# A GRU behind an attention layer: attention regrouped into units of four heads, steps begun after 32 tokens, feed-forward last

## The reference

```python
y   = gelu(x @ W.T + fc_bias + low_rank(f, x) + cond)            # (4, 256, 128)
q, k, v = y @ Wq, y @ Wk, y @ Wv                                  # 16 heads of 64
s   = (q.k + q.rel_emb[clip(i - j, -64, 64) + 64]) / 8            # position term per (i, j)
x   = x + (softmax(s) @ v) @ Wo + bo
# GRU over the 256 tokens, 4 sequences side by side
z   = sigmoid(x_t @ W_z + h @ U_z + cond @ C_z + b_z)
r   = sigmoid(x_t @ W_r + h @ U_r + cond @ C_r + b_r)
hh  = tanh(x_t @ W + (r * h) @ U + cond @ C + b)
h   = (1 - z) * h + z * hh                                        # history H
# feed-forward: the best of 8 experts of width 64 per token, rw = sigmoid(top logit)
out = x + sum_e mask_e * ((rw*H @ up_e.T) * silu(rw*H @ gate_e.T)) @ down_e.T
```

## Time and profile before

| | |
|---|---|
| median of 3 runs | 716.01 us (714.69 to 716.34) |
| span of the profiled execution | 712.3 us |
| median less that span | 3.7 us |
| busy PE, PEld | 623.2, 511.6 us |
| busy DVE, ACT, POOL | 461.2, 323.5, 177.9 us |
| mean granted PE clock | 0.973 |

### The profile page before, as it was taken

How to read it: one execution, slowest core, us unless ns; L and a number is a source line. 1 busy time by engine, 2 the same in 40 slices (tenths; PEclk the granted TensorE clock), 3 DMA queues, 4 the chain that set the end, 5 groups by cost and what they waited for, 6 DMA issues and landing times.

```text
span 712.3 us, 26221 instructions
## 1 busy us (share of the span) xinstructions
PE 623.2 (87%) x7909; PEld 511.6 (72%) x7909; DVE 461.2 (65%) x3362; ACT 323.5 (45%) x1253; POOL 177.9 (25%) x789
## 2 busy tenths in 40 slices
PE   5998888879888898989898989898888889999995
PEld 3445766658778777777787877777777677777864
DVE  1434666636777777777777777777766567766763
ACT  2355666623455555455555554555442223232221
POOL 1012444402332332333332323333211011111110
PEclk8999999977999999999999999999999999999996
DMA  8022555420222222222222222222210000000000
GB/s 231 3 82 59 145 154 140 132 67 25 74 74 69 66 66 66 66 71 71 68 70 68 66 66 66 67 75 66 74 25 2 2 2 6 7 5 4 5 8 6
DMA packets 47805, 43.08 MB, mean 60 GB/s; under 512 B 9340, under 2 KB 47496, under 8 KB 47624
## 3 DMA queue, kind: packets, MB, share of 16 engines
q1 hardware_dynamic: 47168, 40.76, 21.6%
q10 hardware_dynamic: 584, 1.64, 0.7%
HBM read 20.95 MB, written 21.43 MB: 59 GB/s over the span
## 4 chain that ended last, share of the span: by engine, by line
PE 59%; DVE 18%; issue 13%; ACT 7%; DMA 1%; DVEq 1%; SPq 1%; ACTq 0%; POOLq 0%; POOL 0%
PE bank L627 13%; PE bank L640 13%; PE bank L428 7%; PE bank L412 7%; DVE s_sb L850 4%; DVE o_sb L873 3%; ACT hh L770 3%; PE bank L445 2%; DVE g L1001 2%; DVE q L993 2%; ACT oT L656 2%; PE bank L460 2%; PE bank L532 2%; PE bank L462 2%; PE bank L458 2%
## 5 line engine op out<-in xcount | busy, mean ns | idle before, releaser
L360 POOL COPY x_nat<-d 128x4 f32 (+1 forms) x256 | 53.5, 209 | 391.8 <-DVE d L1006 391.8
L640 PE MATMUL bank<-q,uc 128*128 128x54 f32 (+1 forms) x512 | 106.2, 289 | 43.4 <-DVE q L993 41.0
L640 PEld LDWEIGHTS bank<-q,uc 128*128 128x128 f32 x512 | 77.7, 190 | 90.5 <-DVE q L993 85.8
L627 PE MATMUL bank<-g,uw 128*128 128x54 f16 (+1 forms) x2560 | 118.9, 189 | 3.6 <-DVE g L1001 3.6
L760 ACT ACTIVATE trz<-bank 128x8 f32<-128x8 f32 x256 | 45.5, 178 | 167.5 <-PE bank L627 167.2
L627 PEld LDWEIGHTS bank<-g,uw 128*128 128x128 bf16 x2560 | 103.3, 97 | 17.0 <-DVE g L1001 7.8
L627 PE MATMUL bank<-b,uw 128*128 128x54 f16 (+1 forms) x2560 | 110.1, 188 | 0.0
L627 PEld LDWEIGHTS bank<-b,uw 128*128 128x128 bf16 x2560 | 108.1, 103 | 1.1 <-issue 0.2
L770 ACT ACTIVATE hh<-bank 128x4 f32<-128x4 f32 x256 | 44.4, 174 | 135.6 <-PE bank L640 131.2
L1001 DVE TENSOR_TENSOR g<-z,hh 128x4 f16<-128x4 f32 x256 | 41.9, 164 | 97.4 <-ACT hh L770 97.4
L325 POOL COPY qa<-qT 64x64 f32 (+1 forms) x256 | 60.6, 237 | 102.3 <-PE bank L403 63.4
(11 more groups left out here) (133 smaller groups left out, 1025.4 us busy)
## 6 DMA issues: line engine op xcount, KB each, us to landing
skew<-e_sb SPq DMA_DIRECT2D x128, 159.5 KB, 2.2
pos<-skew SPq DMA_DIRECT2D x256, 64.0 KB, 2.4
wkv_sb<-in_L_attn_Wkv ACTq DMA_DIRECT2D x1, 1024.0 KB, 8.3
x_nat<-in_x SPq DMA_DIRECT2D x1, 512.0 KB, 4.5
wq_sb<-in_L_attn_Wq ACTq DMA_DIRECT2D x1, 512.0 KB, 6.0
wo_sb<-in_L_attn_Wo SPq DMA_DIRECT2D x1, 512.0 KB, 7.5
out<-y_out SPq DMA_DIRECT2D x8, 64.0 KB
ffn_nat<-in_L_ffn_w_gate SPq DMA_DIRECT2D x1, 256.0 KB
```

The lines of the kernel that those rows point to most:

```text
L627: ins = mm(out_, uw[:, gate, use, j, :], operand, start=False, stop=True, skip_group_check=True)
L640: mm(c_cols(k, n), uc[:, :], st["q8"][:, now, 0:n], start=False, stop=True, skip_group_check=True).then_inc(c_pre, 1)
```

## The change

Nearly the whole program is new. What it does:

1. **Weights multiplied ahead.** For each head a, M_a = Wq_a Wk_a^T and VO_a = Wv_a Wo_a (128 x 128 each) are formed once. The scores are then (y M_a) y^T, and the output is (P y) VO_a. The 48 projections, kT and v_sb are gone; what is projected, is projected per 32 tokens ("fills", below).
2. **Units of four heads and 32 tokens** of one sequence: 8 chunks x 4 quads of heads x 4 sequences = 128 units (`unit`). P is scaled by 1/sum before it is transposed (`normalize`). Positions read q, scores read g = y M, both straight from the layout of the fills: the POOL copies qa and qb are gone. Slanted loads are one DMA a unit.
3. **Fills.** Per chunk: 2 of q, 4 of g, 4 of o (the output product); each is 4 fp32 products of 128 columns in one spare bank, placed by a table at 40 places of 16 turns, and emptied by DVE in halves.
4. **Turns.** A turn carries unit n: scores(n), transposes and values of n-1, positions(n+4). Turns -4 to 19 run alone, with the late setup between them (transposes of y and Wv, the VO products, the feed-forward weights); step 0 begins at turn FIRST = 20, when 32 tokens of all sequences are done. From there a turn goes beside two steps, so units end at step 216 and the last output fill at step 222.
5. **A step.** r and z have a bank and a tanh each; no splits, all products fp32 with 4 columns: U_r g and U_r b (the older term, issued in the step before) into r, U_z h into z, U q into c. DVE has q, b, g and the state, which it writes into the history itself; POOL has no part in the steps.
6. **Feed-forward last**: 8 tiles of 32 tokens x 4 sequences, 9 slots each, from step FFN_STEP = 223 on; the last begins after step 255. The gate is ACT's Silu with rw as its scale, in place of tanh and products on DVE. Zero products (`fillers`) are put in only where neither attention nor a tile has work on PE.

```diff
-SPLIT = 4096.0
-PERIOD = 16
-EARLY = 5
-WIDE_BESIDE, WIDE = 54, 60
+CH = 32
+QUADS = 4
+UNITS = QUADS * B
+N_UNITS = NCH * UNITS
+LEAD = 4
+FIRST = 20
+FFN_STEP = 2 * (LAST_TURN - FIRST) + 1
+TILE_STEPS = 9
+PERIOD = [("o", -1, 3), ("q", 1, 0), ("q", 1, 1), ("o", 0, 0), ("g", 1, 0), ("o", 0, 1), ("g", 1, 1), ("g", 1, 2),
+          ("o", 0, 2), ("g", 1, 3)]
+PLACES = [(k, s) for k in range(UNITS) for s in (("Be", "Ao") if k % 2 == 0 else ("Be", "Ao", "Bo"))]
...
+            pool.tensor_scalar(urg[:, :], wu[:, 0, :], 0.5, None, ALU.mult)
+            pool.tensor_scalar(uz[:, :], wu[:, 1, :], 0.5, None, ALU.mult)
+            pool.tensor_scalar(urb[:, :], wu[:, 0, :], -0.25, None, ALU.mult)
...
+            def turn(n, slot):
+                if slot == "Ae" and 0 <= n < N_UNITS:
+                    scores(n)
+                if slot == "Be" and 0 <= n - 1 < N_UNITS:
+                    transpose_p(n - 1)
+                if slot == "Ao" and 0 <= n + LEAD < N_UNITS:
+                    positions(n + LEAD)
+                if slot == "Bo" and 0 <= n - 1 < N_UNITS:
+                    values(n - 1)
+                if (n, slot) in FILL_AT:
+                    fill(*FILL_AT[n, slot])
...
+            for t in range(T):                                   # PE
+                n, odd = FIRST + t // 2, t % 2
+                now, before = t % 2, 1 - t % 2
+                if t >= 1:
+                    pe.wait_ge(g_ok, t)
+                    mm(r_bank[:, gate_cols(t)], urg[:, :], g_sb[:, before, :], ...).then_inc(r_done, 1)
+                    pe.wait_ge(d_ok, t)
+                    mm(z_bank[:, gate_cols(t)], uz[:, :], hist[:, t, :], ...).then_inc(z_done, 1)
+                turn(n, "Ao" if odd else "Ae")
+                tile_work(t, "A")
+                pe.wait_ge(q_ok, t + 1)
+                mm(c_bank[:, gate_cols(t)], uc[:, :], q_sb[:, now, :], ...).then_inc(c_done, 1)
+                if t + 1 < T:
+                    turn(n, "Bo" if odd else "Be")
+                    fillers(t, "B")
+                    pe.wait_ge(b_ok, t + 1)
+                    mm(r_bank[:, gate_cols(t + 1)], urb[:, :], b_sb[:, now, :], ...)
+                tile_work(t, "B")
...
+            def turn(n, slot):                                   # ACT
+                if slot == "V1e" and 0 <= n + LEAD - 1 < N_UNITS:
+                    move_e(n + LEAD - 1)
+                if slot == "V2e" and 0 <= n + LEAD - 1 < N_UNITS:
+                    fill_e(n + LEAD - 1)
+                if slot == "V1o" and 0 <= n - 1 < N_UNITS:
+                    move_pt(n - 1)
+                if slot == "V2o" and 0 <= n < N_UNITS:
+                    exps(n)
...
+                act.activation(tr[:, now, :], r_bank[:, gate_cols(t)], ACT.Tanh, scale=0.5).then_inc(tr_ok, 1)
+                act.activation(tz[:, now, :], z_bank[:, gate_cols(t)], ACT.Tanh, scale=0.5).then_inc(tz_ok, 1)
+                turn(n, "V1o" if odd else "V1e")
+                act.activation(hh[:, now, :], c_bank[:, gate_cols(t)], ACT.Tanh).then_inc(hh_ok, 1)
+                turn(n, "V2o" if odd else "V2e")
...
+            def turn(n, slot):                                   # DVE
+                if slot == "W1e" and 0 <= n - 1 < N_UNITS:
+                    normalize(n - 1)
+                if slot == "W2e" and 0 <= n < N_UNITS:
+                    scores(n)
+                if slot == "W1o" and n in EMPTY_AT:
+                    emptied(*EMPTY_AT[n])
+                if slot == "W2o" and 0 <= n - 1 < N_UNITS:
+                    move_o(n - 1)
+                if slot == "W2o" and 0 <= n < N_UNITS:
+                    invert(n)
...
+                stt(q_sb[:, now, :], tr[:, now, :], 1.0, state, ALU.add, ALU.mult).then_inc(q_ok, 1)
+                stt(b_sb[:, now, :], tz[:, now, :], -1.0, state, ALU.add, ALU.mult).then_inc(b_ok, 1)
+                turn(n, "W1o" if odd else "W1e")
+                stt(g_sb[:, now, :], tz[:, now, :], 1.0, hh[:, now, :], ALU.add, ALU.mult).then_inc(g_ok, 1)
+                dve.wait_ge(g_ok, t + 1)
+                stt(hist[:, t + 1, :], b_sb[:, now, :], -0.5, g_sb[:, now, :], ALU.mult, ALU.add).then_inc(d_ok, 1)
+                turn(n, "W2o" if odd else "W2e")
```

More of the change, by code:

```diff
@@ L183, in build @@
+        sg_ok, um_ok, ah_ok, aT_ok, y_ok = sem("sg_ok"), sem("um_ok"), sem("ah_ok"), sem("aT_ok"), sem("y_ok")
+        stored = [sem("stored0"), sem("stored1")]
         block = ctx.enter_context(nc.Block())
         col = lambda v: v.rearrange("(p a) -> p a", a=1)
[L186 to L191, removed]
@@ L208, in tiles_at @@
[L208 to L223, removed]
@@ L226, in rz_cols @@
[L226 to L242, removed]
+        yT4 = yT[:, :].rearrange("p (b t) -> p b t", b=B)
@@ L297, in _ @@
+            for n in range(N_UNITS + 1):
+                if n < N_UNITS:
+                    store(n)
+                if n >= 1:
+                    load(n - 1)
+            for i in range(TILES):
                 sp.wait_ge(y_ok, i + 1)
-                sp.dma_start(out[:, bass.ds(row, STEPS_TILE), :], y_out[:, :]).then_inc(stored, 16)
-            sp.wait_ge(stored, 16 * TILES)
+                sp.dma_start(out.rearrange("b t d -> t b d")[i * CH:(i + 1) * CH], y_out[:, i % 2, :]).then_inc(stored[i % 2], 16)
@@ L301, in _ @@
+            for s in range(2):
+                sp.wait_ge(stored[s], 16 * TILES // 2)
         @block.gpsimd
@@ L405, in scores @@
[L405 to L419 removed]
+            pe.transpose(bank[4][:, 0:128], rel_nat[:, :, :].rearrange("p a d -> p (a d)"), flip[:, :]).then_inc(rel_pe, 1)
@@ new lines, in own_banks @@
+            def own_banks():
+                for i in range(len(LATE) - 3, len(LATE)):
+                    pe.wait_ge(*late_count(i))
+                pe.wait_ge(zeros_ok, 1)
+                pe.wait_ge(u_ok, 1)
+                for k in range(3):
+                    ins = mm(bank[k][:, :], zeros[:, 0:128], zeros[:, :], start=True, stop=True)
+                ins.then_inc(bits_set, 1)
+            for n in range(-LEAD, FIRST):
+                if n == SEED_TURN:
+                    own_banks()
+                if n == -LEAD + 1:
+                    for j in range(2, BEGIN):
+                        if j == 2:
+                            pe.wait_ge(m_ok, 4)
+                        for p in range(4):
+                            fill(j, p)
+                for i in LATE_TURN.get(n, ()):
+                    late(i)
+                for slot in ("Ae", "Be", "Ao", "Bo"):
+                    turn(n, slot)
@@ L649, in _ @@
+            for t in range(T, TAIL):
+                for slot in "AB":
+                    tile_work(t, slot)
         @block.scalar
@@ new lines, in _, with again @@
+            for n in range(-LEAD, FIRST):
+                for i in LATE_TURN.get(n, ()):
+                    late(i)
+                for slot in ("V1e", "V2e", "V1o", "V2o"):
+                    turn(n, slot)
+                if n in (SEED_TURN, SEED_TURN + 1, SEED_TURN + 2):
+                    act.wait_ge(bits_set, 1)
+                    act.wait_ge(late_act, LATE.index("gv") // 2 + 1)
+                    seed(n - SEED_TURN, slice(0, 512))
+            def again(t, gate):
+                if t // CH in range(1, 5) and t % CH == 4 + gate:
+                    seed(gate, chunk_cols(t // CH - 1))
@@ L777, in _ @@
+            for t in range(T, TAIL):
+                for slot in ("V1", "V2"):
+                    tile_work(t, slot)
         @block.vector
@@ new lines, in turn @@
+            def turn(n, slot):
[9 more added lines that the diff above has]
+                    invert(n)
+            for n in range(-LEAD, FIRST):
+                for i in LATE_TURN.get(n, ()):
+                    late(i)
+                for slot in ("W1e", "W2e", "W1o", "W2o"):
+                    turn(n, slot)
@@ L1025 @@
+            for t in range(T, TAIL):
+                for slot in ("W1", "W2"):
+                    tile_work(t, slot)
 _INS = ['x', 'fside_Bx1x1024x16_0', 'cond_1024', 'L0_cond_W', 'L0_cond_fc_bias', 'L0_attn_Wq', 'L0_attn_Wkv', 'L0_attn_Wo',
```

1301 lines of the change are left out of this document (593 added, 708 removed).

## The result

| | before | after |
|---|---|---|
| median beside each other | 716.17 us | 1024.83 us (1017.0 to 1029.06) |
| ratio | | 1.4325 [1.4246, 1.4404] |
| span of the profiled execution | 712.3 us | 1021.8 us |
| mean granted PE clock | 0.973 | 0.549 |
| first tanh of r, last one | | 103.61, 1006.92 us |

What follows compares the result with a forecast made beforehand. Bound by what lies ahead of step 0 and by the step, set by its loop and PE's order. 97 + 443 + 74 + 1.3 + 2 + 13 = 630.3 us span; with 3.7 more, 634 us; range 606 to 692.

Steps and rivals of the forecast that it cites:

- rival C: Steps beside attention: without wide columns the clock falls, 3.5 us a step; 779 us with 100 such steps; chance 0.08.
- step 0: Everything ahead of the first step: it starts at 97 us, where it was at 160; bounds 88 and 112.
- the rest to the last tanh of r: After the steps beside attention: 74 us for the last 40 steps, 1.3 for Silu's load, 2 for ACT's seeds.
- The half clock in the thin turns: Ahead of the first step: a stretch at half clock, counted as 3 us.
- the sum of 2.32: One turn alone: P's copy (0.44), values, their copy, reciprocal, normalize, transposes; 2.32 us, taken as 2.4.
- The step beside attention: Steps 0 to 215: even 1.965, odd 1.91 or 2.135, plus 3%: 2.05 us each, 443 us for 216.
- The even step's wait: Even step beside attention: PE's transposes wait for normalize, queued behind b on DVE, and start at 1.31 us.
- Rival A: Steps beside attention: PE's order is the bound, 0.25 us more a step, 2.3 us, 688 us total; chance 0.14.
- Steps 216 to 255: The last 40 steps: loop alone 1.71 us, with fills and tiles 1.85 us each, 74 us; bounds 1.75 and 2.15.
- Silu: Feed-forward gate on ACT: one table load if Tanh shares its table, 1.3 us; bounds none to 20.5 us.
- B: Feed-forward tiles: Silu and Tanh in different tables, 16 loads less one, 19 us more, 653 us; chance 0.05.
- the six signs: Profile after: first tanh near 97, inputs 32.8 us apart, PE over 90% busy, two waits, PEclk 1.00, three table loads.

Runs made afterwards that it cites:

- e2: The kernel before with its two narrow-product widths, 54 and 60 columns, set to 4, nothing else: 874.83 us, ratio 1.2227.
- e1: The kernel after with the four narrow products of a step on 60 columns, 56 of them zeros, in place of 4: 670.3 us, ratio 0.937.
- e5: e1 plus products of zeros on PE before the positions of turns -3 to -1: 655.03, 655.34, 664.93 and 666.83 us.
- e8: e1 plus zeros in turns -3 to -1, wider zeros from step 216, Silu's table loaded at step 218, a fill product ahead of the transposes: 648.46 us, ratio 0.9077.

## Why the prediction was wrong, step by step

**The failed step** is the sentence on rival C: "in both stages with steps it stayed at 2.4 GHz (0.99 and 1.00), with PE busy 89 and 91%, and in my schedule PE is no less busy". Busy share was read as what holds the clock. The runs show it does not: PE busy 100% at 0.50 (after, 500 to 600), 98% at 0.50 (e2) and 99.7% at 1.00 (e1). What both stages of before had in common with one another, and not with the change, were the wide products, and I had listed their removal in the same paragraph "for" the rival. The pair e1 and after, 670.3 and 1024.8 us, is the price of those columns. With the clock at 0.5 the turn's PE work doubles and PE's order is all that is left of the step, as C had it.

**With the clock held** the rest can be judged on e1, span 666.5 against a forecast of 630.3:

| term | forecast | e1 | |
|---|---|---|---|
| step 0 | 97 | 103.4 | +6.4 |
| 216 steps beside attention | 443 | 459.0 | +16.0 |
| the rest to the last tanh of r | 77.3 | 90.9 | +13.6 |
| behind it | 13 | 13.2 | +0.2 |

Against the kernel before, e1's gain is in the first term (160.1 to 103.4 us), and 2.5 us behind the last step. From the first to the last tanh it takes 549.9 us for 536.5. A step beside attention is hardly shorter (2.125 for 2.16), there are 216 of them for 176, and the last ones are longer (2.33 for 1.98).

- *Step 0.* The half clock in the thin turns, taken as 3 us, lasted from 28 to 57 us in the kernel after (0.52 over 28.4:57.0), and the first turns took up to 5.6 us; with the clock held there, e5's step 0 comes 8.3 us earlier. Ahead of it PE had been idle from 26.7 to 28.4 us. A turn at full clock was mostly 2.9 us, not 2.4: in e1 the exps start at 87.22 and 90.12. Of the 0.58 over the sum of 2.32, 0.31 is in the first link. Between the transposes and the values PE has, in its order, two fill products and the positions, so the values load 0.75 behind the start of ACT's copy of P (86.94), which had 0.44 in the sum. The weight loads of that turn, and the two operations of DVE behind the values:

```profile
86.63 0.30 PEld L396 LDWEIGHTS bank<-yT,m_sb 128*128 128x128 f32 x2
87.05 0.29 PEld L427 LDWEIGHTS bank<-rext,qT 64*128 64x128 f32 x2
87.47 0.30 PEld L399 LDWEIGHTS bank<-oT,vo_sb 128*128 128x128 f32 x2
87.69 0.53 PEld L450 LDWEIGHTS bank<-pt_sb,y_nat 128*128 128x128 f32 x4
...
88.44 0.38 DVE L845 COPY oT<-bank 128x128 f32<-128x128 f32 x1 [0.67 <-PE bank L450]
88.67 0.16 DVE L832 RECIPROCAL rinv<-rsum 128x1 f32<-128x1 f32 x1
88.95 0.35 DVE L838 TENSOR_SCALAR pn_sb<-p_sb,rinv 128x256 f32<-128x256 f32 x1
```

  The other way round, the 16 products for M cost 2.06 us and not 3.6.
- *The step beside attention*, 2.05. In e1 the even step has a mean of 2.01 for 1.965. The odd one is 2.13 in most turns without a fill product in B and 2.35 in most with one, for 1.91 and 2.135: 0.22 over, in both. The term that was too small is positions. They load 0.37 behind z (298.07, 298.44), for 0.22, and keep PE 0.42 (298.44, 298.86), for 0.23: 0.34 more together, of which the 0.13 that the schedule left before the values takes a part, and 0.21 is left. The even step's wait is as drawn: normalize starts 0.08 behind b in 105 of 106 turns, and the transposes wait 0.21, for 0.20. That e8's mean, 2.056, is the forecast 2.05 is luck: its even step is shorter than in the schedule, by the fill product in that wait, and its odd one is longer. Rival A's 0.25 came from one short step; by the means of the two stages it is 0.18.
- *Steps 216 to 255.* 2.33 for 1.85. Taken one by one between two tanh of r, with the granted clock of each: 30 of e1's 39 steps are at 1.00 and have a mean of 2.04, from 1.85 where there is little tile work to 3.03 at the Silu load; 9 have half clock in them, with a mean of 3.32. So of the 0.48, 0.19 is schedule, with the load in it, and 0.29 is clock.
- *Silu.* One load, and three in all, as said; B is out. Its price was more than its length. ACT's timeline in e1:

```profile
582.42 0.17 ACT L782 ACTIVATE tr<-bank 128x4 f32<-128x4 f32 x1 [0.72 <-PE bank L603]
583.57 1.28 ACT L772 ACT_TABLE_LOAD   x1
584.86 0.69 ACT L772 ACTIVATE sg<-bank,rw 128x512 f32<-128x512 f32 x1
585.45 0.17 ACT L782 ACTIVATE tr<-bank 128x4 f32<-128x4 f32 x1
```

  The next tanh of r comes 3.03 us after the last one: the load and the 0.69 of the first Silu lie in the loop together. There is no idle time ahead of the load, and Silu starts 0.01 us behind it, so the drain that the Trainium skill, "ScalarE: Activation LUTs", "What ACT_TABLE_LOAD costs", adds to it isn't seen here.
- *Behind the last step*, 13: 14.9 in the kernel after (1006.92 to 1021.8, clock 0.81 there), 13.2 in e1.
- *What would show it*: of the six signs PEclk and the distance of inputs failed, and step 0 came 6.6 us late, inside its bounds. PE over 90% busy and the three table loads came as said, and are as true of a kernel of 1025 us as of one of 670: a sign that doesn't tell the forecast from its rival is no sign. The waits weren't there in the kernel after, where neither transposes nor values find PE idle from 120 us on; in e1 the transposes' wait for normalize is there, and the values load right behind the c product (299.07, 299.30), without one.
- *The chance.* C spoke of the one resource on which every term of the sum rests, and rows at either side (0.70 and 0.52 in the earlier trace rows) showed it to be unstable. It should have had some 0.3, and the range with it.

## What to carry to other kernels

When a change narrows PE's products, price the whole stage at 1.2 GHz and give that case a real chance; a busy PE is no argument against it. If narrow products must stay, widen them with zero columns first: at full clock a product kept PE 0.22 us with 60 columns as with 4. Then look at the clock stage by stage: 32 columns held it beside attention and not with the tiles. Read PEclk before any other line of the page after: where it is 5, look there before you explain the time by a wait.

## What the runs showed of the hardware

- The granted clock fell from 1.00 to 0.50 in about 1 us (0.97 in 114:115, 0.50 in 115:116) with PE busy without a gap on both sides, and was at 0.50 or near it until 1000 us, with PE busy all the time.
- An fp32 product of 128x128 weights keeps PE 0.22 us with 4 columns (loads at 104.92, 105.14, 105.36 in the kernel after) and with 60 (302.33, 302.55, 302.78 in e1), and 0.42 to 0.43 with 4 at the low clock. In a step the width costs little: 2.10 us with 32 columns, 2.125 with 60.
- Once at 0.50, the clock didn't come back in 700 us of steps on 4 columns, with PE 97% busy (e2, 157 to 857 us), where the same kernel with 54 had it back some 10 us behind its first step.
- A product of 132 columns on 64 of the 128 rows that is followed by one on 128 rows keeps PE 0.42 us (87.05, 87.47 in e1), for 0.23 on 128 rows; sixteen of 128 columns on alternating halves took 0.13 each (e1):

```profile
18.53 2.06 PE L415 MATMUL bank<-wkT,wqT 64*128 64x128 f32 x32
```
